# Both convolutions of the first stage as sixteen 32 by 32 tiles of the array instead of block-diagonal 128 by 128 matmuls

## The reference, cut to what matters

```python
B, T, DIM, HEADS, CF = (4, 2048, 512, 16, 4)        # T is 2048, four sequences
def _compress(z, w, bias):                            # w: (512, 32, 4)
    y = conv_general_dilated(z.transpose(0, 2, 1), w, window_strides=(CF,), padding='VALID',
                             feature_group_count=HEADS)
    return (y + bias[None, :, None]).transpose(0, 2, 1)
q, k, v = split(layernorm(x) @ Wqkv, 3)
k, v = _compress(k, conv_w, conv_b), _compress(v, conv_w, conv_b)
# null key and value in front, causal softmax attention, projection, real part of a 2-D FFT;
# beside it 64 routed experts (8 per token) and a shared expert, all added to x
```

## Time and profile before

| | us |
|---|---|
| median of 3 runs | 5554.69 (5550.97 to 5558.72) |
| the profiled execution | 5551.73 |
| its span, first to last instruction | 5550.0 |
| its PE busy | 5400.4 (97% of the span) |
| its mean granted TensorE clock | 0.989 of full |

### The profile page before, as it was taken

One profiled execution on the slowest core, in us unless ns is written; L12 is line 12 of the kernel. 1 busy time (PEld: TensorE's weight loads), 2 busy tenths in 40 slices (PEclk: granted clock), 3 DMA queues, 4 the chain that ended last, 5 costly groups with the idle time before them and its releaser, 6 DMA issues. The chain is left out here.

```text
span 5550.0 us, 101177 instructions
## 1 busy us (share of the span) xinstructions
PE 5400.4 (97%) x32816; PEld 4528.2 (82%) x32816; DVE 3930.5 (71%) x7327; ACT 2584.3 (47%) x3753; POOL 2998.8 (54%) x2620
## 2 busy tenths in 40 slices
PE   8999989999999999998999999999999999999999
PEld 7888866666666666666999999999999999999886
DVE  7777767777777777776666666666666676667666
ACT  2222223333334333333666666666666666666410
POOL 1222212565555555311777777777777777777514
PEclk9999999999999999999999999999999999999999
DMA  6555454444444444343667777677787667676748
GB/s 220 179 179 179 171 164 131 116 130 125 118 134 122 135 116 130 114 132 106 131 120 149 134 145 157 134 155 175 170 209 173 133 130 161 134 157 112 167 159 289
DMA packets 475980, 832.20 MB, mean 150 GB/s; under 512 B 56212, under 2 KB 157317, under 8 KB 473134
## 3 DMA queue, kind: packets, MB, share of 16 engines
q1 hardware_dynamic: 334894, 538.05, 30.3%
q0 software_dynamic: 140928, 292.13, 29.5%
HBM read 499.54 MB, written 330.47 MB: 150 GB/s over the span
## 5 line engine op out<-in xcount | busy, mean ns | idle before, releaser
L1701 POOL DMA_INDIRECT mid_base<-e_rows,e_ox x556 | 1177.2, 2117 | 368.1 <-POOL e_ox L1696 262.6
L1812 DVE TENSOR_TENSOR e_wgu_lo<-e_wgu,e_wgu_hi 128x2048 fp32r<-128x2048 f32 x278 | 637.3, 2293 | 805.0 <-ACT e_wgu_hi L1735 723.8
L1689 POOL DMA_INDIRECT e_xg<-mid_xn,e_ix x556 | 621.8, 1118 | 338.7 <-POOL e_ix L1686 228.7
L1748 ACT CAST e_xT_hi<-e_ps_t 128x512 fp32r<-128x512 f32 x556 | 298.9, 590 | 924.4 <-PE e_ps_t L1878 924.4
L1025 POOL DMA_INDIRECT mid_ids<-b_pairs,b_cell x512 | 611.4, 1194 | 149.0 <-issue 148.1
L1891 PE MATMUL e_ps_g<-e_xT_hi,e_wgu_hi 128*128 128x256 f32 x2224 | 652.4, 293 | 1.7 <-issue 1.7
L1891 PE MATMUL e_ps_g<-e_xT_lo,e_wgu_hi 128*128 128x256 f32 x2224 | 629.6, 283 | 0.0
L1891 PE MATMUL e_ps_u<-e_xT_hi,e_wgu_lo 128*128 128x256 f32 x2224 | 629.4, 283 | 0.0
L1891 PE MATMUL e_ps_u<-e_xT_hi,e_wgu_hi 128*128 128x256 f32 x2224 | 629.4, 283 | 0.0
L1891 PE MATMUL e_ps_u<-e_xT_lo,e_wgu_hi 128*128 128x256 f32 x2224 | 629.4, 283 | 0.0
L1891 PE MATMUL e_ps_g<-e_xT_hi,e_wgu_lo 128*128 128x256 f32 x2224 | 629.3, 283 | 0.0
(11 more groups left out here) (283 smaller groups left out, 13330.7 us busy)
## 6 DMA issues: line engine op xcount, KB each, us to landing
b_xT_hi<-mid_xT_hi SPq DMA_DIRECT2D x32, 1024.0 KB
b_xT_lo<-mid_xT_lo SPq DMA_DIRECT2D x32, 1024.0 KB
mid_base<-b_x SPq DMA_DIRECT2D x32, 1024.0 KB
e_wgu<-in_gate_w SPq DMA_DIRECT2D x62, 512.0 KB
e_wgu<-in_up_w SPq DMA_DIRECT2D x62, 512.0 KB
e_wd<-in_down_w SPq DMA_DIRECT2D x62, 512.0 KB
ec_cell<-mid_base SPq DMA_DIRECT2D x88, 256.0 KB, 5.1
b_q<-mid_q_hi SPq DMA_DIRECT2D x84, 256.0 KB
```

What stands on the lines that cost most here:

```text
L1689: pool.indirect_dma_start(xg[s][:, i, :], None, t["xn"], bass.IndirectOffsetOnAxis(ap=ix[s][:, i:i + 1], axis=0))\
L1701: pool.indirect_dma_start(t[f"base{i}"], bass.IndirectOffsetOnAxis(ap=ox[s][:, i:i + 1], axis=0), rows[s][:, i, :], None, compute_op=ALU.a ...
L1748: act.copy(xT_hi[s][:, i * DC // 2 * RB:(i + 1) * DC // 2 * RB], ps_t[i][:, :]).then_inc(xT_hi_ready, 1)
L1812: dve.tensor_tensor(wgu_lo[s][:, :], wgu[s][:, :], wgu_hi[s][:, :].bitcast(F32), ALU.subtract)\
```

## The change

The convolutions become 64 matmuls each, one for every tap, chunk and head, with 32 by 32 weights: head `h` reads rows `h*32` onwards, chunk `k` writes output partitions `k*32` onwards, so that each of 16 (chunk, head) pairs has its own tile of the array. Head `h` writes bank `h` of the `xT` banks, keys in columns 0 to 127 and values (`vt`) in columns 128 to 255. The compressed keys stay in that order of channels (partition = chunk and channel, middle axis = head), in SBUF, in memory and in stage B's loads. Values come out as channels by tokens, get their bias on ACT (`vT`), are turned by four PE transposes into a ring bank, and are copied by ACT to `vcs`, which puts the channels back in order. The weights are 128 by 512 instead of 128 by 2048 numbers; one load of a bias, 128 by 512, goes.

```diff
-RING = ([("router", 0)] + [("qkv", i) for i in range(12)] + [("kc", 0), ("vc", 0), ("pos", 0)])
+RING = ([("router", 0)] + [("qkv", i) for i in range(12)] + [("pos", 0), ("vc", 0)])
+RING_LAST = {b: g for g, b in RING_BANK.items()}
...
-        wconv = sb("a_wconv", [P, DC, CF, P])
-        kbias = sb("a_kbias", [P, DC])
-        vbias = sb("a_vbias", [P, DIM])
+        wconv = sb("a_wconv", [P, DC, CF, DH])
+        bias = sb("a_bias", [P, HPC])
...
@@ SP
-                    sp.dma_start(dst[:, :, bass.ds(s * CPB, CPB)].rearrange("c p n -> p c n"), src).then_inc(kc_out, 16)
+                    sp.dma_start(dst[:, :, bass.ds(s * CPB, CPB)], src).then_inc(kc_out, 16)
@@ ACT, behind split_x
                 act.wait_ge(filled["kc"], nth("kc", s, 0))
+                act.wait_ge(filled["vt"], nth("vt", s, 0))
...
-                for k in range(DC):
-                    last_i = act.activation(kcs[:, k, :], bank[RING_BANK[("kc", 0)]][:, k * CPB:(k + 1) * CPB], ACT.Identity,
-                                            bias=kbias[:, k:k + 1])
+                for h in range(HPC):
+                    last_i = act.activation(kcs[:, h, :], bank[h][:, 0:CPB], ACT.Identity, bias=bias[:, h:h + 1])
                 last_i.then_inc(emptied["kc"], 1)
+                if not first:
+                    act.wait_ge(filled["vc"], nth("vc", s - 1, 0))
+                for h in range(HPC):
+                    last_i = act.activation(vT[:, h, :], bank[h][:, CPB:2 * CPB], ACT.Identity, bias=bias[:, h:h + 1])
+                last_i.then_inc(emptied["vt"], 1)
+                act.wait_ge(filled["vc"], nth("vc", s, 0))
+                if not first:
+                    act.wait_ge(vc_out, 16 * s)
+                act.copy(vcs[:, :].rearrange("p (k h o) -> p h k o", k=DC, h=HPC),
+                         bank[RING_BANK[("vc", 0)]][:, :].rearrange("p (h k o) -> p h k o", h=HPC, k=DC))\
+                    .then_inc(emptied["vc"], 1)
@@ DVE, behind split_x
-                dve.wait_ge(filled["vc"], nth("vc", s, 0))
-                if not first:
-                    dve.wait_ge(vc_out, 16 * s)
-                dve.tensor_tensor(vcs[:, :], bank[RING_BANK[("vc", 0)]][:, :], vbias[:, :], ALU.add)\
-                    .then_inc(emptied["vc"], 1)
@@ PE, in transposes, ahead of the first
+                        if not isinstance(s, int) or s > 1:
+                            pe.wait_ge(emptied["kc"], nth("kc", s - 2, 0))
+                            pe.wait_ge(emptied["vt"], nth("vt", s - 2, 0))
@@ PE, behind the qkv groups
-                b = bank_free("kc", 0, s, first)
-                pe.wait_ge(emptied["qkv"], nth("qkv", s, 7))
+                pe.wait_ge(emptied["xT"], nth("xT", s if last else s + 1, DC - 1))
                 if first:
                     pe.wait_ge(late_w_in, 16)
-                for k in range(DC):
+                for kind, src, done, at in (("kc", ks, 7, 0), ("vt", vs, 11, CPB)):
+                    hold(pe, emptied["qkv"], nth("qkv", s, done), passed)
                     for c in range(CF):
-                        last_i = pe.matmul(b[:, k * CPB:(k + 1) * CPB], wconv[:, k, c, :], ks[:, k, c, :], start=c == 0,
-                                           stop=c == CF - 1)
-                last_i.then_inc(filled["kc"], 1)
-                b = bank_free("vc", 0, s, first)
-                pe.wait_ge(emptied["qkv"], nth("qkv", s, 11))
-                for k in range(DC):
-                    for c in range(CF):
-                        last_i = pe.matmul(b[:, k * P:(k + 1) * P], vs[:, k, c, :], wconv[:, k, c, :], start=c == 0,
-                                           stop=c == CF - 1)
-                last_i.then_inc(filled["vc"], 1)
+                        for k in range(DC):
+                            for h in range(HPC):
+                                head = slice(h * DH, (h + 1) * DH)
+                                last_i = pe.matmul(bank[h][k * DH:(k + 1) * DH, at:at + CPB], wconv[head, k, c, :],
+                                                   src[head, k, c, :], start=c == 0, stop=c == CF - 1)
+                    last_i.then_inc(filled[kind], 1)
                 b = bank_free("pos", 0, s, first)
...
                 last_i.then_inc(filled["pos"], 1)
+                b = bank_free("vc", 0, s, first)
+                pe.wait_ge(emptied["vt"], nth("vt", s, 0))
+                for h in range(HPC):
+                    last_i = pe.transpose(b[:, h * P:(h + 1) * P], vT[:, h, :], ident[:, :])
+                last_i.then_inc(filled["vc"], 1)
```

More of the change, by code:

```diff
@@ L135, in load @@
             sp.dma_start(self.kc[i * DH:(i + 1) * DH, :, :].bitcast(F32),
-                         t["kc_" + part][0, :, 0:NC].rearrange("(h r) n -> r h n", r=DH)).then_inc(self.loaded, 16)
+                         t["kc_" + part][0:DH, :, 0:NC]).then_inc(self.loaded, 16)
         sp.dma_start(self.vc[:, :, :], t["vc"][0:NC, 0:P].rearrange("(n p) d -> p n d", p=P)).then_inc(self.loaded, 16)
@@ L148, in prepare @@
         dve.tensor_copy(self.null_heads[:, :], scratch[0:KN, 0, 0:P])
-RING = ([("router", 0)] + [("qkv", i) for i in range(12)] + [("kc", 0), ("vc", 0), ("pos", 0)])
+RING = ([("router", 0)] + [("qkv", i) for i in range(12)] + [("pos", 0), ("vc", 0)])
 RING_BANK = {g: 4 + i % 4 for i, g in enumerate(RING)}
+RING_LAST = {b: g for g, b in RING_BANK.items()}
 ROUTED = EXPERTS + HEADS
-A_PER = {"xT": 4, "router": 1, "qkv": 12, "kc": 1, "vc": 1, "pos": 1}
+A_PER = {"xT": 4, "router": 1, "qkv": 12, "kc": 1, "vt": 1, "vc": 1, "pos": 1}
 def stage_a(nc, t, early):
@@ L184, in stage_a @@
         vs = sb("a_vs", [P, DC, CF, CPB])
-        kcs = sb("a_kcs", [P, DC, CPB])
-        kc_hi = sb("a_kc_hi", [P, DC, CPB], F32R)
+        kcs = sb("a_kcs", [P, HPC, CPB])
+        kc_hi = sb("a_kc_hi", [P, HPC, CPB], F32R)
+        vT = sb("a_vT", [P, HPC, CPB])
         vcs = sb("a_vcs", [P, DIM])
@@ L268, in nth @@
             return step * A_PER[kind] + i + 1
-        NLOADS = 10
+        NLOADS = 9
         block = ctx.enter_context(nc.Block())
@@ L283, in _ @@
             load_x(0)
-            for dst, src in ((ident, t["ident"]), (trif, t["tri"]), (mhalf, t["mhalf"]), (kbias, t["conv_b_col"]),
-                             (vbias, t["conv_b_row"]), (ebias, t["e_bias_row"]), (number, t["e_number_row"])):
+            for dst, src in ((ident, t["ident"]), (trif, t["tri"]), (mhalf, t["mhalf"]), (bias, t["conv_b_col"]),
+                             (ebias, t["e_bias_row"]), (number, t["e_number_row"])):
                 sp.dma_start(dst[:, :], src).then_inc(w_in, 16)
@@ L292, in _ @@
             load_wq(1)
-            sp.dma_start(wconv[:, :, :, :], t["conv_bd"]).then_inc(late_w_in, 16)
+            sp.dma_start(wconv[:, :, :, :], t["conv_w"]).then_inc(late_w_in, 16)
             sp.wait_ge(wq_lo_ready, 1)
@@ L642, in bank_free @@
                 elif not first:
-                    k, o = RING[g + len(RING) - 4]
+                    k, o = RING_LAST[RING_BANK[(kind, i)]]
                     pe.wait_ge(emptied[k], nth(k, s - 1, o))
@@ L899, in load_kv @@
                     sp.dma_start(kc[r][i * DH:(i + 1) * DH, :, :].bitcast(F32),
-                                 t[part][c, :, b * NC:(b + 1) * NC].rearrange("(h r) n -> r h n", r=DH))\
-                        .then_inc(kv_in[r], 16)
+                                 t[part][c * DH:(c + 1) * DH, :, b * NC:(b + 1) * NC]).then_inc(kv_in[r], 16)
                 sp.dma_start(vc[r][:, :, :],
@@ L2266, in internal @@
         xn=d("xn", (TOK + P, DIM)), q_hi=d("q_hi", (DC, P, TOK)), q_lo=d("q_lo", (DC, P, TOK)),
-        kc_hi=d("kc_hi", (DC, P, TOK // CF)), kc_lo=d("kc_lo", (DC, P, TOK // CF)), vc=d("vc", (TOK // CF, DIM)),
+        kc_hi=d("kc_hi", (P, HPC, TOK // CF)), kc_lo=d("kc_lo", (P, HPC, TOK // CF)), vc=d("vc", (TOK // CF, DIM)),
         xT_hi=d("xT_hi", (DC, P, TOK)), xT_lo=d("xT_lo", (DC, P, TOK)), base0=d("base0", (TOK + P, DIM)), base1=d("base1", (TOK + P, DIM)), w8=d("w8", (P, NTILE * TOPK)), pos=d("pos", (P, NTILE * EXPERTS)),
@@ L2283, in layout @@
     conv = a(L0_attn_conv_w).reshape(DC, HPC, DH, DH, CF)
-    conv_bd = np.zeros((P, DC, CF, P), np.float32)
     head_rows = np.zeros((2, HPC, HPC), np.float32)
@@ L2289, in layout @@
     for h in range(HPC):
-        s = slice(h * DH, (h + 1) * DH)
-        conv_bd[s, :, :, s] = conv[:, h].transpose(2, 0, 3, 1)
         head_rows[:, h, h] = 1
@@ L2311, in layout @@
     return dict(
-        x=a(L0_attn_x).reshape(TOK, DIM), wqkv=a(L0_attn_Wqkv), conv_bd=conv_bd,
-        conv_b_col=np.ascontiguousarray(a(L0_attn_conv_b).reshape(DC, P).T), conv_b_row=rows(L0_attn_conv_b),
+        x=a(L0_attn_x).reshape(TOK, DIM), wqkv=a(L0_attn_Wqkv),
+        conv_w=np.ascontiguousarray(conv.transpose(1, 3, 0, 4, 2).reshape(P, DC, CF, DH)),
+        conv_b_col=np.ascontiguousarray(a(L0_attn_conv_b).reshape(DC, HPC, DH).transpose(0, 2, 1).reshape(P, HPC)),
         null_k_row=rows(L0_attn_null_k), head_rows=head_rows.reshape(2 * HPC, HPC),
```

## The result

Slower, by 0.7%. The changed kernel takes 5591.34 us in the median of 4 runs (5588.33 to 5602.8), the one before 5554.72 (4 runs, 5550.97 to 5558.72): a ratio of 1.007, 95% interval 1.0052 to 1.0087. The forecast was 5543. The profiled executions differ by the same: 5588.33 less 5551.73 is 36.6 us.

A forecast was written before the change was run, and what follows sets the result against it. PE, busy 5400.4 of 5550.0 us, was taken as the bound. Steps -10, start -0.7 and end -1.8 made -12 against 5551.73: 5540, or 5543 as median; own range 5521 to 5560, over the cases 5520 to 5625.

The forecast's parts named there:

- What bounds the kernel: Whole kernel: PE, busy 5400.4 of 5550.0 us, is the limit, so a change must shorten PE's list.
- The record pace: Tiled convolutions in stage A: 256 records at 7 ns each, 31 ns the other end, instead of 64 at 112 ns.
- the 0.65 us: Forecast net gain in each of 15 stage A steps: -2.05 us from the earlier router, +1.4 us for the clock.
- Mode switches: Into and out of the tiled convolutions, one visit a step: 0.25 us for both changes together, between 0 and 0.5.
- ACT's eight pieces: ACT after `split_x` adds the bias to four pieces of keys and four of values: 2.2 us, 436.1 to 438.3.
- The gap behind `pos`: PE idle 2.6 us a step, 435.75 to 438.4, waiting on ACT's `emptied["vt"]` before turning the values.
- The turns: PE's four transposes of the values ahead of the next router: 0.104 us each, 438.4 to 438.8.
- What the idle time costs: PE's gap each stage A step lowers the granted clock: a loss of 1.4 us a step, bounds 0 and 3.1.
- Small parts: Moved work on DVE and ACT covered; start -0.7 us from the dropped bias load; last step's end -1.8 us.
- It does not do what it says: Rival: convolutions shrink but the low clock takes 2 us or more a step; 0 to +14, 5555 to 5569; chance 0.08.
- Instructions don't come fast enough: Rival: the 256 records run at 28.6 ns each; +60, 5615; chance 0.28, together with four tiles abreast.
- The clock stays: Rival: PE's gap doesn't lower the clock, 43.9 us router to router; -33, 5521; chance 0.14.

## Why the prediction was wrong, step by step

- *What bounds the kernel.* Held: PE's list is what counts, and the time came by way of PE alone.
- *The record pace*, taken at 7 ns: 13.2 ns. Eight records that lay ready were taken for the pace of 256; the first 32 do keep to 7.7 ns, the rest do not. Both ends named for it, 7 and 31, hold it. That the loss would begin at 10 ns and use up the 0.65 us at 13 was about right.
- *Mode switches*, 0.25 us: 1.82 - 1.70 = 0.12 at the end and 0.32 - 0.23 = 0.09 at the start, 0.21 together. Right.
- *ACT's eight pieces*, 2.2 us: 2.18 (451.58 to 453.76). *The gap behind `pos`*, 2.6 us: 1.89, since the convolutions end 1.5 us later than forecast and ACT begins when they end. *The turns*, 0.104 us each: 0.59 us for the four (453.90 to 454.49), 0.15 each. Together the router came 0.96 us earlier, not 2.05.
- *What the idle time costs*: the largest miss. I took 1.4 us a step, with bounds of 0 and 3.1, from gaps in stage B that had cost 3.4 us of low time. Measured: 40.4 us in 15 steps, 2.7 on average, inside the bounds but twice the term, and 3.24 or 4.83 in each step in which it fell at all. The direction was right (the clock falls at a gap of this size, and it was called the step against the change), the size was not. The ten gaps of stage B held the warning: two showed 6.8 us. PE was busy all the time outside its gap (43.20 + 1.89 = 45.09), which was to help the clock, and it fell all the same. I took the mean of ten gaps, where a fixed pattern of work repeats one case 15 times and may well repeat a long one.
- *Small parts.* Start, -0.7: -0.67. End, -1.8: +3.0. Of the 4.8 between them, 1.5 are the slower pace and 1.6 the idle time amid `vt`'s records; the rest was not taken apart, beyond a POOL subtraction (L373) that took 2.13 us there. The first pass of the loop was 46.63 us, 0.68 longer than before, with idle time of the same kind.

Sum of the misses against the forecast of -12: clock 40.4 - 21 = +19.4; pace and turns, 13 x 1.2 = +15.6; the first two steps +3.5; the end +4.8; later stages +5.4; together +48.7, and -12 + 48.7 = +36.7 us, as measured. Without any low clock it would be 36.7 - 40.4 = -4, much as the run with the gap filled shows it (0.9994, 3 us less than before), so the half clock is what makes the change a loss. Its wrong size alone is not: with the clock at 21 and the rest as measured it would be +17, with the pace as forecast and the clock as measured +21. The two failed steps of the prediction are the clock term and the record pace.

*The rivals.* "It does not do what it says" is the one that came true: the convolutions shrank by 3.6 us a step and the half clock took more than the step had won. Its price, 0 to +14, was too low, and not for the clock: its upper end had 3.1 us a step, 46.5 in all, above the 40.4 measured. It lacked the slower pace, the first two steps, the end and the later stages, 15.6 + 3.5 + 4.8 + 5.4 = 29.3. "Instructions don't come fast enough" had the right place (256 records) and a pace of 28.6 ns, twice the real one. "The clock stays" would have been 45.09 us a step, not 43.9, and it is what the fillers bought. The time lies within the range over the cases, 5520 to 5625, and outside the forecast's own.

The rule of the Trainium skill, "TensorE: Matmul & The Clock Gate", under "Wait — 56ns, not 53.3ns?", that starts are never closer than some 25 ns, does not hold for these tiles: 128 records follow each other after 13.2 ns.

## What to carry to other kernels

A wait of TensorE of about 2 us, placed in a loop, costs its own length and, in two passes of three or in nearly all, 3 to 5 us on top, lost to the half clock (in this kernel, at gaps of 1.89 to 2.28 us): look also at what the worst case in the trace would cost, not only at the mean, and before a change is dropped for it, move independent PE work in front of the wait. Here that turned +0.6% into -0.7% with the same instructions. A block-diagonal convolution is worth splitting into the array's 16 tiles, but what is saved is half of its time, not three quarters: the records cost 13 ns each over the whole group, not the 7 of the first ones.

## What the runs showed of the hardware that I had not expected

- Filler work on TensorE pays: four matmuls of 512 columns whose result is thrown away, in a gap of 1.9 us, took 0.7% off the changed kernel (ratios to the kernel before of 1.0064 and 0.9994).
- The granted clock, by the size of the gap: whole at 0.78 us, nearly always whole at 1.59, low in two of three steps at 1.89, low in nearly all at 2.18 and 2.28. The low time comes in three sizes, 3, 7 and 10 us, and not in proportion to the gap. At 1.89 us two low steps are followed by one that isn't, mostly.
- Tiled fp32 records of 32 by 32 with a weight load each go out every 13.2 ns at 128 columns, in either order of the tiles, the first 32 of a group every 7.7 ns; at 64 columns it is 10.9 ns on average.
- In the first and the last step, which are written out, and in the first pass of the loop, PE stood idle once, for 0.8 to 1.9 us, amid the short records of all kernels with both convolutions tiled, with no wait that the profile shows; in later passes of the loop it did not. That the instructions had not arrived is the likely reading, and no run tested it.
